# A 1-core decoder layer: small scale steps moved from VectorE to GpSimd and ScalarE, and the first expert rows transposed into another PSUM bank

## What is computed

```python
def _bitlinear(x, w):                       # used with Wi, Wf, Wg and Wo
    xn = x * rsqrt(mean(x * x) + 1e-5)
    s = 127.0 / clip(max(abs(xn)), 1e-5, None)          # one scale for each token
    xq = clip(round(xn * s), -128, 127) / s
    ws = 1.0 / clip(mean(abs(w)), 1e-5, None)
    wq = clip(round(w * ws), -1, 1) / ws
    return xq @ wq.T
# 1. gated scan over the tokens of a sequence, per channel
i = silu(_bitlinear(x, Wi)) * (1 - f);  f = sigmoid(_bitlinear(x, Wf))
h = scan(h = f * h + i);  g = _bitlinear(x, Wg)
o = rmsnorm(g) * g_norm_weight * silu(h)
x = layernorm(x + _bitlinear(o, Wo))
# 2. one of four experts for each token, chosen by its token id
x = layernorm(x + (silu(x @ C[e].T) * (x @ C[e].T)) @ C[e].T)
# 3. eight factor matrices, summed first
x = layernorm(x + (x @ sum(factors)) / sqrt(8) + bias)
```

## Time and profile before

| | |
|---|---|
| median of 3 runs | 373.16 us (370.56 to 374.07) |
| time of the profiled execution | 369.25 us |
| its span, first to last instruction | 367.5 us |
| mean granted TensorE clock | 0.92 |
| TensorE busy | 285.9 us (78%) |
| ScalarE busy | 230.8 us (63%) |
| VectorE busy | 225.3 us (61%) |
| GpSimd busy | 200.5 us (55%) |

### The profile page before, as it was taken

The page is one execution under the profiler, slowest core; times in us unless marked ns, Lnnn a source line. Parts: engine busy times, 40 slices in busy tenths (PEclk is TensorE's granted clock), DMA queues, the critical chain, the costliest instruction groups (busy, mean ns, idle before and its releaser), DMA issues.

```text
span 367.5 us, 5728 instructions
## 1 busy us (share of the span) xinstructions
PE 285.9 (78%) x1506; PEld 215.5 (59%) x1518; DVE 225.3 (61%) x488; ACT 230.8 (63%) x456; POOL 200.5 (55%) x381
## 2 busy tenths in 40 slices
PE   1376467575687997998998895999399999999960
PEld 1254235242575675676876674777288888888640
DVE  4799999999387579839656753452234444444420
ACT  4779877977367696777777666256145555555441
POOL 2455867858546348466565837546044444444542
PEclk9998859695599999999999999899799999999996
DMA  8999968753883530003012101201401111100000
GB/s 261 389 387 374 228 117 160 143 138 89 198 162 62 94 115 2 29 40 105 0 48 75 54 29 77 69 29 42 131 29 57 52 38 59 57 30 24 28 7 0
DMA packets 17406, 37.02 MB, mean 101 GB/s; under 512 B 1503, under 2 KB 1631, under 8 KB 17376
## 3 DMA queue, kind: packets, MB, share of 16 engines
q0 software_dynamic: 6496, 15.74, 18.6%
q1 hardware_dynamic: 10880, 20.92, 17.2%
HBM read 26.68 MB, written 10.76 MB: 102 GB/s over the span
## 4 chain that ended last, share of the span: by engine, by line
PE 36%; POOL 6%; issue 6%; DMA 5%; ACT 4%; DVE 3%; POOLq 0%; ACTq 0%; DVEq 0%; SPq 0%
PE bank_m L1264 4%; PE bank_m L1268 4%; PE bank_m L1265 4%; PE bank_z L1264 3%; PE bank_z L1265 3%; DMA sorted_rows<-r,place 3%; PE bank_z L1268 3%; PE bank_y L1264 3%; PE bank_y L1265 3%; PE bank_y L1268 3%; DMA rows<-sorted_rows 2%; POOL n_d L313 2%; PE bank_tr L1235 2%; PE bank_q L1235 2%; POOL x L353 1%
## 5 line engine op out<-in xcount | busy, mean ns | idle before, releaser
L312 POOL TENSOR_SCALAR n_v<-n_dev 128x1 f32<-128x1 f32 (+1 forms) x46 | 10.1, 220 | 60.9 <-ACT x L626 28.5
L1264 PE MATMUL bank_y<-c_hi,h_hi 128*128 x76 | 32.2, 424 | 3.1 <-ACT h_hi L594 1.5
L1264 PE MATMUL bank_z<-c_hi,a_hi 128*128 x76 | 32.8, 432 | 1.9 <-ACT a_hi L594 1.9
L1264 PE MATMUL bank_m<-f_hi,m_hi 128*128 128x512 f32 x76 | 31.6, 416 | 3.4 <-DVE f_lo L876 2.6
L895 DVE TENSOR_TENSOR act_z<-bank_z,act_z 128x512 f32<-128x512 f32 x19 | 13.1, 691 | 34.3 <-ACT act_z L608 34.3
L358 POOL DMA_INDIRECT out<-r,token_of x19 | 20.6, 1087 | 23.1 <-ACT r L633 19.9
L1265 PE MATMUL bank_z<-c_lo,a_hi 128*128 x76 | 31.7, 417 | 0.0
L1265 PE MATMUL bank_y<-c_lo,h_hi 128*128 x76 | 30.8, 405 | 0.0
L313 POOL TENSOR_TENSOR n_d<-n_v,minus_half 128x1 f32<-128x1 f32 (+1 forms) x46 | 28.3, 615 | 3.8
L1265 PE MATMUL bank_m<-f_lo,m_hi 128*128 128x512 f32 x76 | 30.1, 396 | 0.0
L353 POOL TENSOR_TENSOR x<-x,bias_b 128x512 f32<-128x512 f32 x19 | 25.0, 1315 | 9.0 <-PE bank_q L1235 8.8
(11 more groups left out here) (205 smaller groups left out, 855.6 us busy)
## 6 DMA issues: line engine op xcount, KB each, us to landing
f_sum<-in_factors POOLq DMA_DIRECT2D x7, 1024.0 KB, 10.6
rows<-sorted_rows SPq DMA_DIRECT2D x19, 256.5 KB, 2.9
xs<-in_x SPq DMA_DIRECT2D x8, 512.0 KB, 6.2
c_stage<-in_ctx_t SPq DMA_DIRECT2D x4, 1024.0 KB, 14.3
sorted_rows<-pad_row SPq DMA_DIRECT2D x1, 1539.0 KB, 20.6
w_stage<-in_wf_t SPq DMA_DIRECT2D x1, 1024.0 KB, 8.4
w_stage<-in_wi_t SPq DMA_DIRECT2D x1, 1024.0 KB, 10.6
w_stage<-in_wg_t SPq DMA_DIRECT2D x1, 1024.0 KB, 12.8
```

What stands on the lines that cost most here:

```text
L1264: t.matmul(bank[:], hi[:, c, :], w_hi(c), start=(c == 0), stop=False)
```

## The change

Four things change; the arithmetic keeps its form, with 1/x by a power of -1 on GpSimd where VectorE used a reciprocal.

1. For groups 2 to 7 the four instructions of `scale_x` leave VectorE. `power_x` on GpSimd makes them instead, as five (one product is split in two). They stand where `power_x(g)` stood, at the end of turn `g - 2`.
2. `quantise_o` of groups 0 and 1 (turns 1 and 2) goes from VectorE to ScalarE, where it stands between `max_row` and `x_by_channel`.
3. At the start `quantise_x(1)` and `order_slots` go ahead of the first `weight_scale` on VectorE. On GpSimd `number_slots` goes ahead of the first `weight_ready`, and `add_factor(1)` goes behind `places` and `scale_g(0)`.
4. `transpose_a(0)` writes to `bank_q`, which is free once `o_by_channel(2)` is done, and no longer waits for `residual_1(2)`. On ScalarE `high_a(0)` stands ahead of `square_1(2)`.

```diff
+        def x_links(g):
+            return 2 * (g + 1) if g < 2 else 5 * (g + 1) - 6
...
                 def power_x(g):
...
                     link(pool.tensor_tensor(x_r[:, i, :], x_ve[:], minus_half[:], ALU.pow), s.xch)
+                    if g < 2:
+                        return
+                    pool.wait_ge(s.mxx, GT * g + GT)
+                    pool.wait_ge(s.qx, GT * (g - 1))
+                    pool.wait_ge(s.mcb, g - 1)
+                    link(pool.tensor_tensor(x_mr[:], x_max[:, i, :], x_r[:, i, :], ALU.mult), s.xch)
+                    link(pool.tensor_scalar(x_mc[:, i, :], x_mr[:], GUARD, None, ALU.max), s.xch)
+                    link(pool.tensor_tensor(x_rc[:, i, :], x_mc[:, i, :], minus_one[:], ALU.pow), s.xch)
+                    pool.tensor_tensor(x_rq[:], x_rc[:, i, :], x_r[:, i, :], ALU.mult).then_inc(s.x_rq, 1)
+                    pool.wait_ge(s.x_rq, g - 1)
+                    pool.tensor_scalar(x_q[:, i, :], x_rq[:], QMAX, None, ALU.mult).then_inc(s.xq_s, 1)
...
+                def quantise_o(p):                                   # ScalarE
+                    act.wait_ge(s.oq_s, p + 1)
+                    act.wait_ge(s.mxo, GT * p + GT)
+                    act.wait_ge(s.half_magic, 1)
+                    for j in range(GT):
+                        tile = o_tok[:, p % 2, j, :]
+                        a.activation(tile, tile, ACT.Identity, bias=half_magic[:], scale=o_q[:, j:j + 1]).then_inc(s.qo, 1)
...
                     max_row(g + 1)
+                    if turn < MERGE:
+                        quantise_o(p)
                     x_by_channel(g + 1)
...
+                high_a(0)
                 square_1(MERGE - 1)
-                high_a(0)
                 norm_1(MERGE - 1)
...
+                    elif n == 0:
+                        pe.wait_ge(s.oqt, MERGE)
+                        rows_by_channel(bank_q, rows[:, n % RING, 0:D], s.ta)
```

More of the change, by code:

```diff
@@ L167, in decoder_layer @@
             chosen tiles next_fill through gains orders numbers events slot_sel slot_mm slot_off place route route_dve
[L168 removed]
+            sqx mxx xch x_mr x_mc x_rc x_rq xq_s half_magic g_c qx tx xqt mcb mce zf zi df di tanh silu fe ii scan sh
             zg sqg gg gch g_f ts o mxo sqo och o_a oq_s qo to oqt wo r mean1 sq1 n1 b1 x1 number scat0 scat1
@@ L414, in _ @@
                 weight_ready(W_G)
-                add_factor(1)
                 places()
                 scale_g(0)
+                add_factor(1)
                 power_x(2)
@@ L596, in high_a @@
                 def high_a(n):
-                    high(n, bank_a if n > TAIL - 1 else bank_tr, a_hi, s.ta, s.z, s.tah)
+                    high(n, bank_a if n > TAIL - 1 else bank_tr if n else bank_q, a_hi, s.ta, s.z, s.tah)
                 def high_h(n):
@@ L884, in low_a @@
                 def low_a(n):
-                    low(n, bank_a if n > TAIL - 1 else bank_tr, a_hi, a_lo, s.tah, s.z, s.tal)
+                    low(n, bank_a if n > TAIL - 1 else bank_tr if n else bank_q, a_hi, a_lo, s.tah, s.z, s.tal)
                 def low_h(n):
@@ L995, in _ @@
                 scale_x(1)
+                quantise_x(1)
+                order_slots()
                 weight_scale(W_F)
                 round_weights(W_F)
-                order_slots()
                 weight_scale(W_I)
@@ L1001, in _ @@
                 rescale_f(0, 0)
-                quantise_x(1)
                 rescale_f(0, 1)
@@ L1032, in _ @@
                     max_o(p, 1)
-                    scale_x(g + 1)
                     quantise_x(g + 1)
@@ L1040, in _ @@
                     gate_i(g, 1)
-                    quantise_o(p)
+                    if turn == MERGE:
+                        quantise_o(p)
                     scans(g, 1)
```

22 lines of the change are left out of this document (11 added, 11 removed).

## The result

The changed kernel takes 377.13 us (median of 20 executions, 372.06 to 382.69), the kernel before 373.31 (20 executions, 370.46 to 375.89). The ratio is 1.0067, with an interval of 1.0036 to 1.0099: slower, where 372.8 us and "within 1%" had been forecast. That ratio counts only executions within 1.5% of each kernel's fastest; the medians of all give 1.0102, and the changed kernel's executions lie twice as far apart (10.6 us instead of 5.4). The profiled execution took 374.0 us with a span of 371.9, against 369.25 and 367.5 before.

A forecast was written before the change was run, and what follows sets the result against it. VectorE was taken as the fullest engine in turns 1 to 3, then a chain over TensorE, first norm, scatter and load; -0.8 (second slot's rows) -0.8 (turn 5) +1.2 (clock) = -0.4, so 372.8 us; range 369.4 to 375.0.

The forecast's parts named there:

- ScalarE had waits of that size there, so I let TensorE's `project_back(0)` start when it did: Turn 1: quantising o adds 1.4 us net on ScalarE, taken to fit its waits, leaving the start of `project_back(0)` unchanged.
- in turns 1 to 3 the steps fall into waits of GpSimd that are there already: GpSimd: the five scale steps, 2.0 us for a group with the power, would be hidden by existing waits.
- Just in time: GpSimd before turn 1: scale of group 2 needed by about 40.1, with `x_q(2)` there at 39.5.
- the landing of `add_factor(1)`: Factor DMA on GpSimd: issued at 35.1, landing between 44.1 and 51.4, taken as 48; `add_factor(2)` near 48.5, as now.
- still at about 57.9: Sign in turn 2: GpSimd issues `add_factor(3)` at about 57.9, as in the kernel before.
- rival D: `add_factor(1)` lands at 51.4, turn 2 comes 2.2 us later, time +1.4 to 374.6 us; chance 0.13.
- VectorE's idle time before `gate_i` in turn 2 above 1 us: Sign in turn 2: VectorE waits over 1 us ahead of `gate_i`, released by ScalarE.
- What VectorE loses: Turns 1 to 3: `scale_x` and `quantise_o` take 3.9 us off VectorE; the moves at the start count as nothing.
- The first slot: After turn 3: scatter 0.7 us earlier, transposes at 91.6, `up(0)` about 93.3, second slot's rows 0.8 us early.
- if ScalarE waits for the first rows with `square_1(2)` behind it: Sign at the first slot that would show the prediction wrong; the rows' load had been taken as 3.1 us.
- The clock: TensorE, turn 4: a 4.0 us wait lowers the clock, losing 1.9 us, 0.7 covered, so 1.2 us given back.
- Turn 5: `scale_x` leaves VectorE ahead of `f_lo`, for which TensorE waits: 0.8 us gained.

The follow-up runs named there:

- a2: The changed kernel with `add_factor(5)` moved behind `number_rows(2)`, so issued after the load of the first rows: 1.0084 of before.
- a3: The changed kernel with `square_1(2)` back ahead of `high_a(0)` on ScalarE: 1.0051 of before.
- d4: The kernel before with only `add_factor(1)` moved behind `places` and `scale_g(0)`: 1.0069 of before.
- g1: `d1` with `add_factor(3)` moved behind `power_1(0)` on GpSimd in turn 2: 1.0049 of before.
- a0: The changed kernel unedited, measured again on the chip of the second series: 1.0281 of before.
- d1: `a3` with turn 1 as before: scale of group 2 and quantising of the first o tiles on VectorE: 1.0114 of before.
- c2: The kernel before with the fourth part of the change and the sixth and seventh factor DMAs moved later: 0.9922 of before.

## Why the prediction was wrong

**Two steps failed, and each alone would make turn 2 late.**

**The first is turn 1.** "ScalarE had waits of that size there, so I let TensorE's `project_back(0)` start when it did" was wrong by 4.2 us: it started at 54.67 instead of 50.46. Behind it stands "in turns 1 to 3 the steps fall into waits of GpSimd that are there already". The five steps for group 2 fell into none. They pushed the o scale back by 1.9 us, further into VectorE's rounding of W_O, where it was stretched by another 1.5. The prediction had asked only whether the five steps would be stretched, not those behind them. "Just in time" failed too: `x_q(2)` came at 41.4 instead of 39.5, since the first steps of `places` were slow beside VectorE's scans (0.57 us instead of 0.31) and `places` ended at 35.6 instead of 34.2. VectorE waited 1.21 us for it. In the first profile the last `n_mean` of turn 1 is 1.9 us late and that of turn 2 1.65, with no wait for `n_b` between. This rests on the traces (the first profile, `a2`, `a3`). No run has the late turn 1 with the factor chain cut, so its price by itself stays open.

**The second is the landing of `add_factor(1)`.** The prediction had it issued at 35.1 and took 48 out of 44.1 to 51.4, "`add_factor(2)` then goes out near 48.5, as now". It was issued at 36.81 and took 13.6 us: 50.4. Of the 2.4 us too much, 1.7 are the late issue and 0.7 the duration. In the 13 profiles with the later place it landed between 50.2 and 52.1, after 13.4 to 15.3 us. `add_factor(2)` went out at 50.92 and `add_factor(3)` at 60.50, not "still at about 57.9". That is the path of rival D, which had been worked out (2.2 us late in turn 2, from a landing later than 48.5) and given a chance of 0.13. `d4` and `g1` show it from both sides, and in `a0`, the same kernel as in the first profile, it sets turn 2. In the first profile it does not: the forecast sign "VectorE's idle time before `gate_i` in turn 2 above 1 us" is absent there, and in `a0` it is 1.79 us.

**What VectorE loses** did leave VectorE, and in `d1` turn 1 ends earlier than before, perhaps by the work moved into the early wait, which had been costed at nothing.

**The first slot.** Its scatter was to be 0.7 us earlier and was 1.6 later. First transposes at 93.88 instead of 91.6, `up(0)` at 95.79 instead of 93.3; the second slot's rows 1.4 us late instead of 0.8 early. Of this place only the text's own warning came true, "if ScalarE waits for the first rows with `square_1(2)` behind it": the load had been given 3.1 us as a fixed price, and in the profiles it is 2.6 to 3.3 or 5.7 to 7.5, with 0.14 us of its issue time between the two. The first profile, near the fastest of its 20 executions, doesn't have this, `a0` has; that the wide spread of the 20 is the race is likely, but no single execution other than the profiled ones shows it.

**The clock** fell as forecast: a wait of 5.86 us (4.0 had been said), 2.5 us lost behind it (1.9 said) and 0.6 of that covered (0.7 said), so 1.9 instead of 1.2. But it was lost at another place: in the projections of the next group, which come ahead of slot 1's `up`. The product of twelve matmuls, for which 4.6 us had been said, took 3.0. The Trainium skill (TensorE: Matmul & The Clock Gate, section on HAM oscillation) says that a wait for a DMA between bursts of matmuls can bring the clock down, and the trace agrees: 0.90 instead of 1.00 in that window.

**Turn 5** gave what was said: from `transpose_h(1)` to the first `mix` the shift shrinks by 0.66 us (0.8 said).

**The sum.** Instead of -0.8 for the second slot's rows it was +1.4, the clock +1.9 instead of +1.2, turn 5 -0.7, and the later hand-overs and the lower clock of the last stretch add some 1.8: 4.4 us of span, 4.75 in the profiled execution.

## What to carry to other kernels

Work taken off the busiest engine makes its neighbours' queues longer, and what stands in those queues ahead of the next hand-over decides. Here there were two such things: the o scale behind five more small steps, and a DMA issue that blocks GpSimd until its predecessor has landed. The 2.0 us for the five steps were counted, their effect on what stands behind them was not. Where two paths are about equally late, mending one gains nothing, and that doesn't show that it was harmless: ask in the trace who waited for whom. So follow each queue on which something is put or reordered, and ask of every wait in it who stands behind. If a small load on the path is issued right behind a large one of no hurry, it can take twice as long, as here: move the large one, as in `c2`, or make sure that nothing in a hurry is queued behind the engine that waits for the load, as in `a3`.
